# Four expert tiles at a time in L1_ffn, and another order of work in the attentions of a twelve-sublayer decoder

## The chip, the cores and the metric

The kernel runs on one core of one Trainium2 chip. TensorE (PE in the profile; PEld is its weight load) multiplies matrices, VectorE (DVE), ScalarE (ACT) and GpSimd (POOL) work on rows of 128 partitions, and SyncE (SP) issues most of the DMAs. The metric is the device time of one execution in microseconds; the kernel before takes 4104.81 us, the median of three runs (4103.65 to 4107.08).

## The reference

The input is 128 sequences of 64 tokens with 128 features, 8192 tokens. Twelve sublayers follow one another, each with the sum and a layer norm around it; everything is float32:

```
x = layernorm(x + sublayer(x))       # 12 times
```

They are, in order: a mixture of 8 experts (moe_first), a single-head cross attention, a feed-forward with ternary weights, the attention with rotary positions and a difference of two softmaxes (diff), a masked cross attention (causal), the mixture of 32 small experts (L1_ffn), the attention with distance biases (alibi), a cross attention with masked keys (keys), a convolution with experts, a gated scan, a cross attention with a full mask (full), and a mixture of 8 experts (moe_last). Five of them share one shape, 16 heads of 8 features over 64 tokens:

```
scores = einsum('bihd,bjhd->bhij', x @ Wq, ctx @ Wk) * scale     # masked or biased
probs  = softmax(scores, -1)
out    = einsum('bhij,bjhd->bihd', probs, ctx @ Wv).reshape(b, s, 128) @ Wo + bo
```

In diff queries and keys are first multiplied by rotary tables, values have 16 features for 8 pairs of heads, and what is normed by its root mean square and goes on is the first softmax's output less lambda times the second's. keys has no Wo. The mixture of small experts, with a hidden layer of 32:

```
e = argmax(x @ router_w.T + router_b)                  # one of 32 experts per token
y = relu(relu(x @ w1[e] + b1[e]) @ w2[e] + b2[e])
```

## The kernel before, in words

Nothing is scheduled by a program: each engine's instructions stand in the order in which the sublayer's function writes them (`body` in a block per engine), and semaphores alone tie the engines together. Sublayers don't overlap.

**Attention** (`attention`, L1047) goes through 16 chunks of 512 tokens, each of four tiles k = 0 to 3 of 128 tokens. Chunk c's tiles are computed while chunk c + 1 is projected, and the output of chunks c - 1 to c - 3 is finished. For tile t, TensorE's `body` (L1345) writes: `scores` of tile t + 1 (4 products on 64x64 quarters of the array, in four of the mask besides); `mix_values` of t - 1 (16 small products of probabilities with values); `turn(t, 0)` (four transposes of the probabilities into the bank pT); at some k a projection (`project` into the banks near and far), `turn_output` or `output`; `turn(t, 1)` into the same bank pT; at some k `project_values` (into near) and `turn_rows` (near). `turn(t, 1)` waits until ScalarE has copied what `turn(t, 0)` wrote. ScalarE's `body` (L1440) writes the copy of `turn(t, 0)`, the copy of `turn(t, 1)`, and both exponentials of tile t + 1 (`exponentials`, L1419). DVE's `body` (L1580) writes `shift_scores` of t + 1 (maximum and difference, twice), `heads_output` of t - 1, and at some k `rope_products` (only diff), `residual`, `moments` and `normalise`. POOL spreads keys over the blocks of heads (`spread_keys`, L1654) and does the small powers.

VP is the number of value projections per chunk: 1, and 2 in diff, where they stand behind tiles 1 and 2, and the rotary products behind tiles 0 and 1. In diff each chunk's output is also normed: ScalarE squares (`square_output`), DVE sums (`mean_squares`), POOL takes the power -1/2 (`rms`, L1677, L1691), and DVE multiplies (`rms_output`, L1556) at the start of the chunk after the next.

**L1_ffn** (`moe_small`, L2204) sorts the tokens by expert in two halves (parts). Each token gets a slot so that a tile of 128 slots has one expert; a half has 32 + 32 = 64 tiles. POOL scatters the rows to slots in DRAM (slot_x) and later gathers the results (slot_y). The loop in between takes a pair of tiles j, 64 pairs in all: SP and ScalarE each load one expert (161 columns: w1, its bias, and w2 with its bias as a 33rd row) into a ring of 8; SP loads the pair's rows three pairs ahead (`load_slots`) and stores the results (`store_slots`); TensorE writes `turn(j + 2)`, `hidden(j + 1)`, `output(j)`; ScalarE copies the transposes and does the first relu; DVE evicts. In L1_ffn the bank of the hidden layer is called rank_ps and that of the output count_ps. SP's part and TensorE's part of the loop:

```
for j in range(ALL):                                    # SP, L2402
    if j + 3 < ALL: load_expert(sp, 2 * (j + 3))
    if j + 3 < ALL: load_slots(j + 3)
    store_slots(j)                                      # waits for the eviction of j
for j in range(-2, ALL):                                # TensorE, L2473
    turn(j + 2); hidden(j + 1); output(j)
```

## Time and profile before

| | |
|---|---|
| median of 3 runs | 4104.81 us (4103.65 to 4107.08) |
| the profiled execution's own time | 4081.88 us |
| its span | 4080.1 us |
| busy in the span | PE 3018.0, PEld 2047.6, DVE 2256.7, ACT 1718.3, POOL 1789.2 us |
| mean granted clock of TensorE | 0.859 |

The profile shows one execution. Its own time lies 1.8 us over its span, and 23 us under the median of the other runs. Busy shares are means over twelve sublayers, so the views below are taken by stretch. A granted clock of 1.00 is 2.4 GHz and one of 0.50 is 1.2 GHz. In a row of the timeline an `x8` means that several like instructions in a row are told as one; a float32 product appears as two records. A name leaves its numbers out: L_ffn is L1_ffn in the stretch from 1753 to 2150 us. The stages that the change touches lie at 935 to 1405 us (diff), 1428 to 1738 (causal), 1753 to 2150 (L1_ffn), 2171 to 2481 (alibi), 2512 to 2824 (keys) and 3404 to 3714 (full).

### The profile page before, as it was taken

To read this page: it belongs to the slowest core of one execution; us is meant where nothing else is said; L and a number is where in the kernel's file an instruction comes from. 1 tells how busy PE (TensorE), PEld (TensorE's weight loads), DVE (VectorE), ACT (ScalarE), POOL (GpSimd) and SP (SyncE) were. 2 spreads that over 40 slices of the span, in tenths; PEclk is the share of its full clock that TensorE was granted. 3 is DMA by queue.
4 is the path that set the end of the run, shared out by engine and by line. 5 is a ranking of instruction groups with operands and counts; after the bars stand their busy time and mean duration, and the time that the engine had idled before them with its cause. 6 is when DMAs were issued, how large, how long until landed. Compare 5 with 4: busy or idle time off the path is not lost. (4 is left out here: it accounts for less than half of the span.)

```text
span 4080.1 us, 81328 instructions
## 1 busy us (share of the span) xinstructions
PE 3018.0 (74%) x27802; PEld 2047.6 (50%) x27802; DVE 2256.7 (55%) x6213; ACT 1718.3 (42%) x3334; POOL 1789.2 (44%) x1575
## 2 busy tenths in 40 slices
PE   3399907767777599946747996886899867997693
PEld 2387805554455356634524664554344434666572
DVE  2002336536777577751235775886777576775123
ACT  0144404334444366602214664664555554662341
POOL 2544272225565455523344554664022354552534
PEclk9999959888998799955558998998898788997896
DMA  6377611020010112114521112221000001221573
GB/s 215 115 227 218 191 41 45 6 7 24 32 41 31 53 55 73 55 41 122 136 76 41 55 53 67 76 86 59 1 1 1 1 3 47 77 67 56 160 224 106
DMA packets 305037, 304.44 MB, mean 75 GB/s; under 512 B 91108, under 2 KB 226821, under 8 KB 304648
## 3 DMA queue, kind: packets, MB, share of 16 engines
q1 hardware_dynamic: 269160, 252.01, 20.1%
q0 software_dynamic: 16384, 33.59, 2.8%
q10 hardware_dynamic: 19232, 15.50, 1.2%
q8 instruction: 147, 2.41, 0.2%
q14 instruction: 114, 0.93, 0.1%
HBM read 161.27 MB, written 55.84 MB: 53 GB/s over the span
## 5 line engine op out<-in xcount | busy, mean ns | idle before, releaser
L802 DVE TENSOR_TENSOR moe_first_tile_y<-moe_first_out_ps,moe_first_expert_w 128x256 f32<-128x256 f32 x78 | 33.1, 425 | 336.5 <-PE moe_first_out_ps L937 336.4
L998 POOL DMA_INDIRECT slot_x<-x_tok,moe_first_slots x128 | 123.7, 967 | 177.8 <-DVE moe_first_slots L775 75.1
L978 ACT ACTIVATE moe_first_hid<-moe_first_hid_ps,moe_first_expert_w 128x256 f32<-128x256 f32 x312 | 128.2, 471 | 155.6 <-PE moe_first_hid_ps L926 155.6
L1012 POOL DMA_INDIRECT moe_first_token_y<-slot_y,moe_first_slots x128 | 123.8, 967 | 100.4 <-issue 65.2
L1665 POOL TENSOR_TENSOR causal_k_blocks<-causal_k_T,headmask 128x1024 f32<-128x1024 f32 x64 | 121.2, 1896 | 105.9 <-PE causal_scores L1277 101.9
L2783 PE MATMUL L_ffn_experts<-L_ffn_expert_w,x_T 128*128 128x512 f32 x256 | 166.2, 735 | 1.8 <-ACT L_ffn_expert_out L2880 1.8
L1665 POOL TENSOR_TENSOR alibi_k_blocks<-alibi_k_T,headmask 128x1024 f32<-128x1024 f32 x64 | 121.2, 1896 | 105.2 <-PE alibi_scores L1277 101.2
L1665 POOL TENSOR_TENSOR full_k_blocks<-full_k_T,headmask 128x1024 f32<-128x1024 f32 x64 | 121.2, 1896 | 93.8 <-PE full_scores L1277 89.5
L937 PE MATMUL moe_first_out_ps<-moe_first_expert_w,moe_first_hid 128*128 128x128 f32 x1248 | 162.2, 281 | 0.0
L1416 ACT ACTIVATE diff_probs_T<-diff_pT 128x512 f32<-128x512 f32 x128 | 76.4, 597 | 183.0 <-PE diff_pT L1291 183.0
L1665 POOL TENSOR_TENSOR keys_k_blocks<-keys_k_T,headmask 128x1024 f32<-128x1024 f32 x64 | 120.7, 1896 | 74.7 <-PE keys_scores L1277 71.1
L937 PEld LDWEIGHTS moe_first_out_ps<-moe_first_expert_w,moe_first_hid 128*128 128x128 f32 x1248 | 150.8, 191 | 5.0 <-issue 0.2
L926 PE MATMUL moe_first_hid_ps<-moe_first_tile_xT,moe_first_expert_w 128*128 128x256 f32 x624 | 149.1, 382 | 0.6 <-ACT moe_first_tile_xT L969 0.6
L2338 DVE COPY L_ffn_tile_y<-L_ffn_count_ps 128x256 f32<-128x256 f32 x64 | 27.2, 425 | 195.8 <-PE L_ffn_count_ps L2466 195.8
L2946 POOL TENSOR_SCALAR L_ffn_ms_eps<-L_ffn_ms 128x4 f32<-128x4 f32 x16 | 3.7, 231 | 290.6 <-DVE L_ffn_ms L2713 290.6
L2705 DVE SCALAR_TENSOR_TENSOR L_ffn_combined<-L_ffn_expert_out,L_ffn_mix,L_ffn_combined 128x128 f32<-128x128 f32 x448 | 128.5, 349 | 4.0
L1665 POOL TENSOR_TENSOR diff_k_blocks<-diff_k_T,headmask 128x1024 f32<-128x1024 f32 x64 | 126.3, 1993 | 9.3 <-POOL diff_k_T L1652 5.6
L1416 ACT ACTIVATE keys_probs_T<-keys_pT 128x512 f32<-128x512 f32 x128 | 76.4, 597 | 114.7 <-PE keys_pT L1291 114.7
L2527 POOL DMA_INDIRECT slot_x<-x_tok,L_ffn_slots x64 | 66.8, 1044 | 131.2 <-DVE L_ffn_tile_y L2338 64.8
L1509 DVE TENSOR_REDUCE diff_maxima<-diff_scores 128x8 f32<-128x512 f32 x128 | 87.0, 680 | 65.0 <-PE diff_scores L1277 65.0
L1416 ACT ACTIVATE causal_probs_T<-causal_pT 128x512 f32<-128x512 f32 x128 | 76.4, 597 | 107.5 <-PE causal_pT L1291 107.5
L1416 ACT ACTIVATE alibi_probs_T<-alibi_pT 128x512 f32<-128x512 f32 x128 | 76.4, 597 | 107.2 <-PE alibi_pT L1291 107.2
(544 smaller groups left out, 9152.3 us busy)
## 6 DMA issues: line engine op xcount, KB each, us to landing
moe_first_expert_w<-in_L_attn_experts SPq DMA_DIRECT2D x78, 578.0 KB, 4.0
moe_last_expert_w<-in_L_ffn_experts SPq DMA_DIRECT2D x46, 578.0 KB, 4.1
slot_x<-blank ACTq DMA_DIRECT2D x2, 4992.0 KB, 44.2
moe_first_tile_x<-slot_x SPq DMA_DIRECT2D x78, 128.0 KB, 4.1
slot_y<-moe_first_tile_y SPq DMA_DIRECT2D x78, 128.0 KB, 1.9
L_ffn_tile_x<-slot_x SPq DMA_DIRECT2D x64, 128.0 KB, 2.3
slot_y<-L_ffn_tile_y SPq DMA_DIRECT2D x64, 128.0 KB, 1.8
moe_last_tile_x<-slot_x SPq DMA_DIRECT2D x46, 128.0 KB, 3.9
```

What stands on the lines that cost most here:

```text
L802: dve.tensor_tensor(y_out[:, q, :, :], out_bank[q][:, 0:SLOT_TILE].rearrange("p (s d) -> p s d", s=SPAN), over(wall[:, j % RING, 2 * FF + ...
L926: last = pe.matmul(hid_bank[h][:, SLOT_TILE * (b % 2):SLOT_TILE * (b % 2) + SLOT_TILE], wall[:, j % RING, 128 * b:128 * b + 128], xT[:, j ...
L937: last = pe.matmul(out_bank[j % 2][:, D * s:D * s + D], hid[:, j % 2, b, TILE * s:TILE * s + TILE], wall[:, j % RING, FF + D * b:FF + D * ...
L978: act.activation(hid[:, j % 2, b, :], hid_bank[b // 2][:, SLOT_TILE * (b % 2):SLOT_TILE * (b % 2) + SLOT_TILE], gelu, bias=wall[:, j % RIN ...
L998: pool.indirect_dma_start(slot_x[part][:, :], bass.IndirectOffsetOnAxis(slots[:, part, r, t:t + 1], 0), net.x_tok[:, part * K + t, :], Non ...
L1012: pool.indirect_dma_start(y_in[:, p, k, r, :], None, slot_y[part][0:NT * SLOT_TILE, :], bass.IndirectOffsetOnAxis(slots[:, part, r, t:t + ...
L1416: act.activation(probs_T[:, t.p, 4 * g:4 * g + 4, :].rearrange("p k t -> p (k t)"), pT_bank[:, :], ACT.Copy)\
L1509: dve.tensor_reduce(maxima[:, t.p, heads], src, AX_X, ALU.max).then_inc(max_done, 1)
L1665: pool.tensor_tensor(k_blocks[:, t.p, :, :], keys.to_broadcast([128, 8, TILE]), lanes.to_broadcast([128, 8, TILE]), ALU.mult).then_inc(spr ...
L2527: pool.indirect_dma_start(slot_x[part][:, :], bass.IndirectOffsetOnAxis(slots[:, part, t:t + 1], 0), net.x_tok[:, part * K + t, :], None). ...
L2705: last = dve.scalar_tensor_tensor(combined[:, p, k, :], expert_out[:, p, k, e, :], w, combined[:, p, k, :], ALU.mult, ALU.add)
L2783: pe.matmul(expert_bank[g][:, :], net.x_T[:, TILE * t:TILE * t + TILE], experts_s[:, 4 * g:4 * g + 4, :].rearrange("p e d -> p (e d)"), st ...
```

## The change

In all five attentions TensorE writes `turn(t, 0)` ahead of `mix_values(t - 1)`, and ScalarE writes the first exponentials of tile t + 1 right behind the copy of `turn(t, 0)`, the second ones behind the copy of `turn(t, 1)`. In diff the value projections stand behind tiles 2 and 3 instead of 1 and 2, and the product with the inverse root mean square is done by POOL right after its power, one chunk earlier than DVE did it.

In L1_ffn four tiles (a quad) are one step. Their four hidden layers are four products on the four column groups of the array (32 columns each) into one bank, their outputs four products on the four row groups (32 rows each) into four banks, with the second bias added by four more products of ones with a row group; one relu with 128 partitions and one eviction of 128x512 follow. An expert's weights come in two loads (w1: 128x32; w2 and biases: 32x257). Slot rows are loaded two quads ahead. The output's banks are no longer doubled: `output(j)` waits for the eviction of j - 1. Nothing else changes.

```diff
@@ attention @@
+    V_AT = PER - VP if lambdas is not None else PER - 1 - VP
@@ project_values, turn_output @@
-                    if wo is not None and c.shift(-2 - late).inside(CHUNKS) and n == VP - 1:
+                    if wo is not None and c.shift(-2 - late).inside(CHUNKS) and n == 0:
                         pe.wait_ge(oT_copied, done(c.shift(-2 - late)))
...
-                            pe.wait_ge(v_copied, nth(c.shift(2 + late), 2 * VP, 2))
@@ TensorE, body @@
                             scores(t.shift(1))
+                        turn(t, 0)
                         if t.shift(-1).inside():
                             mix_values(t.shift(-1))
-                        turn(t, 0)
...
-                        if PER - 1 - VP <= k < PER - 1 and c.shift(1).inside(CHUNKS):
-                            project_values(c.shift(1), k - (PER - 1 - VP))
+                        if 0 <= k - V_AT < VP and c.shift(1).inside(CHUNKS):
+                            project_values(c.shift(1), k - V_AT)
@@ ScalarE, body @@
                         copy_turned(t, 0)
+                        if t.shift(1).inside():
+                            exponentials(t.shift(1), 0)
...
                         copy_turned(t, 1)
                         if t.shift(1).inside():
-                            exponentials(t.shift(1))
+                            exponentials(t.shift(1), 1)
@@ DVE: rms_output and its calls are gone; POOL, rms @@
                     pool.tensor_tensor(rms_inv[:, :], ms_eps[:, :], minus_half[:, :], ALU.pow).then_inc(rms_done, 1)
+                    pool.wait_ge(rms_done, done(c))
...
+                    pool.tensor_tensor(o_heads[:, c.u % 2, :, :].rearrange("p t (k d) -> p (t k) d", k=8),
+                                       o_diff[:, c.u % 2, :, :].rearrange("p t (k d) -> p (t k) d", k=8),
+                                       spread_last(rms_inv[:, :], dv), ALU.mult).then_inc(o_normed, 1)
@@ moe_small @@
-    J = NT // 2
+    J = NT // 4
...
-    RING, XRING = 8, 4
+    RING, XRING = 4, 3
@@ DVE, evict @@
-                    dve.tensor_copy(y_out[:, q, :, :], out_bank[q][:, 0:PAIR].rearrange("p (s d) -> p s d", s=2))\
-                        .then_inc(out_done, 1)
+                    dve.tensor_copy(y_out[:, q, :, :], out_banks[:, :, 0:D]).then_inc(out_done, 1)
@@ load_expert @@
+                eng.dma_start(up[:, j % RING, g, :], w_up[bass.ds(e, 1), :, :].rearrange("o p h -> p (o h)"))\
+                    .then_inc(w_landed[j % RING], 16)
+                eng.dma_start(down[H * g:H * g + H, j % RING, :], w_down[bass.ds(e, 1), :, :].rearrange("o p w -> p (o w)"))\
+                    .then_inc(w_landed[j % RING], 16)
@@ SP @@
                 for j in range(ALL):
+                    if j + 2 < ALL:
+                        load_slots(j + 2)
                     if j + 3 < ALL:
-                        load_expert(sp, 2 * (j + 3))
+                        load_expert(sp, j + 3, 0)
+                    store_slots(j)
                     if j + 3 < ALL:
-                        load_slots(j + 3)
-                    store_slots(j)
...
+                        load_expert(sp, j + 3, 2)
@@ TensorE, hidden and output @@
+                    pe.wait_ge(w_landed[j % RING], 128 * (j // RING + 1))
+                    for g in range(4):
+                        last = pe.matmul(hid_bank[j % 2][H * g:H * g + H, 0:TILE], up[:, j % RING, g, :],
+                                         xT[:, j % 2, TILE * g:TILE * g + TILE], start=True, stop=True)
...
+                    if j >= 1:
+                        pe.wait_ge(out_done, j)
+                    for g in range(4):
+                        lane = slice(H * g, H * g + H)
+                        pe.matmul(out_banks[:, g, 0:D], net.ones[lane, :], down[lane, j % RING, D + 1:W], start=True, stop=False)
+                    pe.wait_ge(hid_done, j + 1)
+                    for g in range(4):
+                        lane = slice(H * g, H * g + H)
+                        last = pe.matmul(out_banks[:, g, 0:D], hid[lane, j % 2, :], down[lane, j % RING, 0:D],
+                                         start=False, stop=True)
@@ ScalarE, relu @@
+                    act.activation(hid[:, j % 2, :], hid_bank[j % 2][:, 0:TILE], ACT.Relu,
+                                   bias=down[:, j % RING, D:D + 1]).then_inc(hid_done, 1)
```

How the order moves, first on SP in the loop of L1_ffn. L_ffn_tile_x is a slot load, slot_y a store, L_ffn_expert_w (then _up and _down) an expert's weights; TENSOR_LOAD reads the expert's number. Before, one turn of the loop ends with the store and the next begins:

```order
L2376 DMA L_ffn_expert_w<-in_L_ffn_experts 128x161
L2389 DMA L_ffn_tile_x<-slot_x 128x2x128
L2395 DMA slot_y<-L_ffn_tile_y 128x2x128
L2375 TENSOR_LOAD L_ffn_expert_of
L2375 ISA x2
L2376 ISA
L2376 DMA L_ffn_expert_w<-in_L_ffn_experts 128x161
L2389 DMA L_ffn_tile_x<-slot_x 128x2x128
```

The same place after the change, a store of quad j and the slot load of quad j + 3 behind it:

```order
L2395 DMA slot_y<-L_ffn_tile_y 128x4x128
L2373 TENSOR_LOAD L_ffn_expert_of
L2373 ISA x2
L2374 ISA
L2374 DMA L_ffn_expert_up<-in_L_ffn_up 128x32
L2376 ISA
L2376 DMA L_ffn_expert_down<-in_L_ffn_down 32x257
L2389 DMA L_ffn_tile_x<-slot_x 128x4x128
```

The slot load stands behind a store in both; before it is that of pair j + 4 behind the store of j, now that of quad j + 3 behind the store of j, with two weight loads in between instead of one.

TensorE in that loop before, where L_ffn_turn_ps is `turn`, L_ffn_rank_ps `hidden` and L_ffn_count_ps `output`:

```order
L2442 MATMUL L_ffn_turn_ps<-ident,L_ffn_tile_x 128x128 x2
L2454 MATMUL L_ffn_rank_ps<-L_ffn_tile_xT,L_ffn_expert_w 32x128 x2
L2466 MATMUL L_ffn_count_ps<-L_ffn_expert_w,L_ffn_hid 128x128 x2
L2442 MATMUL L_ffn_turn_ps<-ident,L_ffn_tile_x 128x128 x2
L2454 MATMUL L_ffn_rank_ps<-L_ffn_tile_xT,L_ffn_expert_w 32x128 x2
```

And after:

```order
L2445 MATMUL L_ffn_turn_ps<-ident,L_ffn_tile_x 128x128 x4
L2456 MATMUL L_ffn_rank_ps<-L_ffn_tile_xT,L_ffn_expert_up 32x128 x4
L2465 MATMUL L_ffn_out_ps<-L_ffn_expert_down,ones 128x128 x4
L2469 MATMUL L_ffn_out_ps<-L_ffn_expert_down,L_ffn_hid 128x128 x4
L2445 MATMUL L_ffn_turn_ps<-ident,L_ffn_tile_x 128x128 x4
```

The order of the three steps is the same; the groups are four instead of two, and the bias group is new.

TensorE in causal, tile 2 of a chunk, before: causal_o_ps is the mixing, causal_pT the transposes of probabilities, causal_near_ps the transposes of the output and then the values' projection.

```order
L1277 MATMUL causal_scores<-causal_k_blocks,causal_q_T 64x512 x4
L1302 MATMUL causal_o_ps<-causal_v_blocks,causal_probs_T 64x18 x16
L1291 MATMUL causal_pT<-ident,causal_probs 128x128 x4
L1322 MATMUL causal_near_ps<-ident,causal_o_heads 128x128 x4
L1291 MATMUL causal_pT<-ident,causal_probs 128x128 x4
L1251 MATMUL causal_near_ps<-causal_wv,causal_cT_in 64x64 x16
```

And after:

```order
L1278 MATMUL causal_scores<-causal_k_blocks,causal_q_T 64x512 x4
L1292 MATMUL causal_pT<-ident,causal_probs 128x128 x4
L1303 MATMUL causal_o_ps<-causal_v_blocks,causal_probs_T 64x18 x16
L1322 MATMUL causal_near_ps<-ident,causal_o_heads 128x128 x4
L1292 MATMUL causal_pT<-ident,causal_probs 128x128 x4
L1252 MATMUL causal_near_ps<-causal_wv,causal_cT_in 64x64 x16
```

The mixing now stands between the two groups of transposes.

## Rows read from the trace of the kernel before

**Rows 1.** The page's first line.
```profile
span 4080.1 us, 81328 instructions
```

**Rows 2.** Busy time by stretch: us, PE, PEld, DVE, ACT, POOL, clock, DMA share, GB/s.
```profile
1428.00:1738.00 310.00, 286.36 (x4085) 192.55 (x4082) 239.16 (x564) 192.17 (x345) 158.06 (x108) 1.00 0.17 61
...
2512.00:2824.00 312.00, 268.61 (x3926) 172.97 (x3926) 248.13 (x564) 187.23 (x333) 187.32 (x123) 0.99 0.21 73
...
1853.00:2088.00 235.00, 187.23 (x672) 118.30 (x672) 50.94 (x168) 67.76 (x200) 70.33 (x78) 0.50 0.48 131
```

**Rows 3.** Waits, whole span: who waited for whom, us in total, times, longest.
```profile
PE keys_pT L1291 <- ACT keys_probs_T L1416: 39.9, 49, 0.9
...
PE causal_pT L1291 <- ACT causal_probs_T L1416: 20.8, 34, 0.8
PE alibi_pT L1291 <- ACT alibi_probs_T L1416: 20.8, 34, 0.8
PE full_pT L1291 <- ACT full_probs_T L1416: 20.8, 34, 0.8
```

**Rows 4.** Timeline, PE, one causal stretch: start us, us, instruction, [idle before].
```profile
1610.51 1.11 PE L1302 MATMUL causal_o_ps<-causal_v_blocks,causal_probs_T 128*64 128x18 f32 x32
1611.55 0.66 PE L1291 MATMUL causal_pT<-ident,causal_probs 128*128 128x128 f32 x4
1612.99 0.63 PE L1291 MATMUL causal_pT<-ident,causal_probs 128*128 128x128 f32 x4 [0.78 <-ACT causal_probs_T L1416]
1613.55 0.41 PE L1272 MATMUL causal_scores<-causal_mask_b,causal_ident_b 64*64 64x512 bf16 x4
1613.79 1.03 PE L1277 MATMUL causal_scores<-causal_k_blocks,causal_q_T 64*64 64x512 f32 x8
...
1622.73 0.63 PE L1291 MATMUL causal_pT<-ident,causal_probs 128*128 128x128 f32 x4
1623.20 0.60 PE L389 MATMUL causal_near_ps<-ident,causal_ln_out 128*128 128x128 f32 x4
```

**Rows 5.** Timelines of PE, DVE, POOL and ACT in one chunk of diff.
```profile
1230.58 1.97 PE L1251 MATMUL diff_near_ps<-diff_wv,diff_xT_in 128*64 128x128 f32 x16 [3.96 <-DVE diff_qk_parts L1500]
...
1216.13 2.17 DVE L1561 TENSOR_TENSOR diff_o_heads<-diff_o_diff,diff_rms_inv 128x512 f32<-128x512 f32 x1 [1.31 <-POOL diff_rms_inv L1691]
...
1233.72 3.75 POOL L1665 TENSOR_TENSOR diff_k_blocks<-diff_k_T,headmask 128x1024 f32<-128x1024 f32 x2 [0.38 <-POOL diff_k_T L1652]
...
1239.55 5.50 POOL L1691 TENSOR_TENSOR diff_rms_inv<-diff_ms_eps,diff_minus_half 128x32 f32<-128x32 f32 x1 [0.24 <-POOL diff_ms_eps L1684]
...
1238.93 1.24 ACT L1407 ACTIVATE diff_v_blocks<-diff_near_ps 64x512 f32<-64x512 f32 x2
```

**Rows 6.** Timeline, all engines, in the expert loop of L1_ffn.
```profile
1901.66 1.22 PE L2466 MATMUL L_ffn_count_ps<-L_ffn_expert_w,L_ffn_hid 33*128 33x128 f32 x4
...
1902.92 0.42 DVE L2338 COPY L_ffn_tile_y<-L_ffn_count_ps 128x256 f32<-128x256 f32 x1 [3.61 <-PE L_ffn_count_ps L2466]
...
1904.51 0.35 SPq L2376 DMA_DIRECT2D L_ffn_expert_w<-in_L_ffn_experts  x1
...
1904.90 0.43 SPq L2389 DMA_DIRECT2D L_ffn_tile_x<-slot_x  x1
...
1907.22 0.69 PE L2442 MATMUL L_ffn_turn_ps<-ident,L_ffn_tile_x 128*128 128x128 f32 x2 [1.26 <-DMA L_ffn_tile_x<-slot_x]
...
1907.84 1.06 PE L2454 MATMUL L_ffn_rank_ps<-L_ffn_tile_xT,L_ffn_expert_w 128*32 128x128 f32 x4
...
1908.83 0.58 PE L2466 MATMUL L_ffn_count_ps<-L_ffn_expert_w,L_ffn_hid 33*128 33x128 f32 x1
```

**Rows 7.** Tile L_ffn_count_ps: ns min/median/max, first and last start.
```profile
L2338 DVE COPY L_ffn_tile_y<-L_ffn_count_ps x64: 424/425/425, 1859.0 to 2087.6; 128x256 f32<-128x256 f32 x64
...
L2307 DVE COPY L_ffn_before_tile<-L_ffn_count_ps x4: 680/686/692, 1791.3 to 1822.6; 128x512 f32<-128x512 f32 x4
```

**Rows 8.** DMA issues: KB each, median us from issue to landing.
```profile
moe_first_tile_x<-slot_x SPq DMA_DIRECT2D x78, 128.0 KB, 4.1
```

More of the change, by code:

```diff
@@ L1461, in _ @@
                     copy_values(first.c, n)
[L1462 removed]
+                for g in range(2):
+                    exponentials(first, g)
                 chunk_turns(act, body)
```

158 lines of the change are left out of this document (66 added, 92 removed).

## The prediction

> **What bounds the kernel now.** I read the page first. Its busy shares are means over twelve sublayers that run one after the other on one core [rows 1], so they say little; the stretches of the five attentions and of the small-expert sublayer come next. In causal, a typical attention, TensorE is busy 286.4 of 310 us at a granted clock of 1.00, with DVE at 239.2: TensorE sets the pace. In keys it is 268.6 of 312 and DVE is nearer, 248.1. In the loop of L1_ffn the clock stands at 0.50 (1.2 GHz), the DMA engines are busy 0.48 of the time, and no engine is full [rows 2]. Then the waits. In causal, alibi, keys and full one wait of TensorE stands out: the second group of transposes waits for ScalarE's copy of the first (both go through one bank), 20.8 + 20.8 + 39.9 + 20.8 = 102.3 us in all [rows 3]. The timeline shows it: mixing starts at 1610.51, the first transposes at 1611.55, and the second ones only at 1612.99 after 0.78 us idle [rows 4]. In diff three things stop the chain: the projection of the next chunk's values waits 3.96 us for the rotary products on DVE, and everything behind it on TensorE waits too, scores included; DVE waits 1.31 us for POOL's power and then takes 2.17 us for the product with it [rows 5].
>
> In L1_ffn the timeline is to be read as a ring [rows 6]. Output of one pair starts at 1901.66. DVE evicts at 1902.92, SP stores, reads an expert's number, issues the expert's load at 1904.51 and the slot load at 1904.90; TensorE starts that load's transposes at 1907.22, having waited for it, the hidden layer at 1907.84 and the output at 1908.83. That is 7.17 us, and two pairs are done in it, since a slot load is issued three pairs ahead. 64 pairs [rows 7] took 235 us [rows 2].
>
> **Attention other than diff.** The mixing (1.04 us from start to start) moves in between the two transposes of a tile. A wait of 0.78 to 0.9 us is then covered whole, wherever it stood; the 102.3 us are the most that can go. What is late next: in causal, alibi and full DVE has 71 us of slack in 310 [rows 2], so I count all of 62.4. In keys DVE is busy 248.1 us, and with the gaps between its dependent instructions some 16.0 us of a chunk of 19; TensorE less its waits needs 16.6. I take 32 of the 39.9. The first transposes now follow the scores at once and so want their exponentials one mixing earlier. ScalarE gives them the first half right after its copy of the first transposes; the shifted scores of that half are ready two DVE instructions after the scores, some 1.4 us, while TensorE has 3.3 us or more of other work before it asks. I cost that at nothing; if DVE falls behind, it comes back tile by tile (rival 3).
> Against it stands one more change of the array's shape in each tile (scores, transposes, mixing, transposes, where it was scores, mixing, transposes). The row: four transposes followed by another full-size group take 0.47 us from start to start (1622.73 to 1623.20), followed by 64x64 ones 0.56 (1612.99 to 1613.55) [rows 4]. I take 0.07 of that difference of 0.09 for each of 5 x 64 tiles, 22 us; bounds 0 and 0.15 (48 us). The Trainium skill, TensorEngine Tiling (Array Packing), section Tiling Modes, says that a change of tiling mode drains TensorE; it gives no price, and these two rows agree in sign. Four sublayers: 62.4 + 32 - 4 x 4.5 = 76 us less; bounds 30 and 102.
>
> **diff.** Removed from DVE, per chunk: the product of 2.17 us and the wait of 1.31 us ahead of it [rows 5]; and, since the values are projected one tile later, TensorE no longer blocks the scores behind them, 3.96 us. Together 7.4 us. Given back, by following one chunk from the end R of its last rotary product: POOL adds the rotary parts and spreads keys (with R at 1230.5 its two spreadings run from 1233.72 to 1237.47; the first, needed for the next chunk's first scores, ends at about R + 5.2 [rows 5]), so these scores end at R + 6.2 while DVE is free at R + 5.4: 0.8 us. In tile 3 TensorE now projects the second half of the values and the transposes of the rows stand right behind it, in the same bank: they wait for ScalarE's copy of the transposes (0.6), an exponential (0.6) and the two copies of values (1.24) [rows 5], so that the following scores end at R + 13.3, where DVE was ready at R + 10.6: 2.7 us. POOL gets the product: a spreading of twice the size takes it 3.75 / 2 = 1.9 us [rows 5], so 0.9 to 1.9, and at most the 2.17 of DVE; I take 1.3. It stands behind the power of 5.50 us, and POOL's next keys come at about R + 16.5, just before TensorE asks at R + 17. Net 7.4 - 0.8 - 2.7 = 3.9 us in this chunk; as its waits are larger than the average (15 of 16 chunks wait), I take 2.8 x 15 = 42 us, less 4 for the change of shape: 38. Bounds: 0 (POOL or the new wait takes it all) and 4.5 x 15 = 68.
>
> **L1_ffn.** Work is halved in count: 32 quads for 64 pairs, one eviction, one slot load, one store, one relu each; two weight loads per tile instead of one. But the order of SP and TensorE closes the ring. SP issues the slot load of quad j + 2 after it has stored quad j - 1; TensorE transposes quad j + 2 directly after the output of quad j - 1. Nothing of TensorE's lies beside the way from output to output any more, and each turn of the ring does one quad. Its terms, at 1.2 GHz:
> - Eviction to slot load: 1904.90 - 1902.92 = 1.98, plus 0.27 for 128x512 instead of 128x256 (686 against 425 ns [rows 7]), plus 0.39 for the second weight issue (1904.90 - 1904.51) [rows 6]: 2.65.
> - Landing of the slot load: 2.32 for 128 KB (1904.90 to 1907.22) [rows 6]; 256 KB are bounded by that and by the 4.1 of the same size in the busier moe_first [rows 8]. I take 3.0.
> - Four transposes: 0.62 is two of them and 0.08 of hand-over [rows 6], so 1.16.
> - Hidden: 0.99 for 512 columns streamed now [rows 6]; 1024 columns, on four column groups. Unshared 2.0; shared in four 0.5. The scores, on four quarters of the array, stream 8 x 512 columns in 1.03 us at 2.4 GHz [rows 4], against 512 in 1.22 us at 1.2 GHz here: groups do run beside each other. I take 0.7.
> - Bias and output: 2048 columns on four row groups. Unshared 4.9 (four times 1.22), shared 1.2; I take 1.4.
> - Hand-overs 0.1.
> Sum 9.0 us a quad against 7.17 for the same four tiles. 29 quads wait in the ring (three loads are issued ahead), the first output and the last two quads add 14 us (three times three groups as above): 29 x 9.0 + 14 = 275 against 235, 40 us more. Bounds: with landing 2.32, hidden 0.5, output 1.2 the ring is 7.9, 243 us, 8 more; with 4.1, 2.0 and 4.9 it is 14.9, 446 us, 211 more. All else hides: ScalarE's four issues and two copies take some 4 us of each 9; POOL's scatter and gathers keep their pace.
> The Trainium skill speaks against this part too: TensorE: Matmul & The Clock Gate, section LDWEIGHTS, says that a weight load costs by its columns, not its rows, so a 32x128 load is as long as a 128x128 one. By its figure, the 16 loads of 128 columns take at least 16 x 107 ns = 1.7 us as an estimate, and the ring 9.3; my 1.4 would be 0.3 short, 9 us in all. No row here shows loads on four row groups.
>
> **Sum.** 4105 - 76 - 38 + 40 = 4031 us; against the profiled execution's own 4082 it would be 4008. That execution ran 23 us under the median of the three runs; I forecast against the median, as the changed kernel will be timed. I say **4030**.
>
> **Rivals.**
> 1. The ring is slower still, and the kernel with it. The groups of hidden and output don't run beside each other at these sizes, and the larger landing comes near 4. Place: the loop of L1_ffn. It decides from (235 + 114 - 14) / 29 = 11.6 us a quad, where the loop eats the 114 us of the attentions. At 14.9 the time is 4105 - 114 + 211 = 4202. For it: only 128 columns per instruction, all unshared bounds. Against: the scores' rows. Chance 0.11.
> 2. The ring isn't what binds: slot loads come in time as SP runs ahead. Then TensorE (3.3 us of groups) and ScalarE (some 4 us of copies and issues) set about 4.4 a quad, 32 x 4.4 + 6 = 147 us, 88 less: 4105 - 114 - 88 = 3903. Against: SP's store stands before the load and waits for the eviction. Chance 0.05.
> 3. The wait moves instead of going: the first transposes wait for exponentials, DVE is the bound, and the four attentions keep their 102 us. 4105 - 38 + 40 = 4107, less what little is saved: 4100. For: DVE at 0.8 of keys. Against: 71 us of slack in the other three. Chance 0.10.
> 4. diff gains nothing, POOL's 5.50 us and the product behind it being the new pace, or the new wait in tile 3 being longer: 4105 - 76 + 40 = 4069. Chance 0.14.
> The forecast itself 0.60, with a range of its own from 3985 to 4085.
>
> **From these to the numbers.** 0.2% is 8 us, about what a measurement can tell here from no change. Faster: 0.58 of the forecast, 0.05, 0.03 of rival 3, 0.13 of rival 4: 0.79. Same: 0.01 + 0.04 + 0.01 and 0.02 of rival 1: 0.08. Slower: the rest, 0.13. Range 3970 to 4110: it leaves out rival 2, most of rival 1 and the forecast's tails.
>
> **What would show it.** TensorE's wait in the second transposes (102.3 us) nearly gone, the four stretches some 15 to 30 us shorter each; no new wait of the first transposes for exponentials of more than a few us. In diff no 4 us wait at the projection of values, and a new one of 1 to 2 us at the transposes of the rows. In L1_ffn DMA waits ahead of every group of transposes, 5 us each, and quads 9 us apart. I am wrong if quads come faster than 7.2 us or slower than 11.6, or if a wait for exponentials fills the place of the old one.

## The result, and the profile after

The changed kernel takes **4087.6 us** (median of 5 runs, 4079.9 to 4091.0), the kernel before on the same chip 4107.0 (5 runs, 4103.7 to 4111.5): ratio 0.9949, interval 0.9935 to 0.9964, **19.4 us less** (15 to 27 by the interval). The forecast was 4030, some 75 us less. The sign was right and the time lies in the range, but three quarters of the gain are missing.

First the stretches, each from the start of an attention's first scores to that of its last. Columns: window, length, busy time (and instructions) of TensorE, its weight loads, DVE, ScalarE and POOL, TensorE's clock, DMA share, GB/s. Before, for causal, keys and diff:

```profile
1430.10:1729.80 299.70, 278.22 (x3976) 185.65 (x3972) 234.47 (x552) 186.44 (x336) 155.96 (x107) 1.00 0.18 62
2514.80:2815.20 300.40, 260.27 (x3808) 166.30 (x3804) 243.43 (x552) 181.17 (x323) 185.09 (x122) 1.00 0.22 74
938.60:1372.80 434.20, 342.64 (x3762) 216.57 (x3764) 336.14 (x688) 197.32 (x351) 258.40 (x147) 0.90 0.09 33
```

The same view after, with alibi, full and the loop of L1_ffn, which answers to the last of [rows 2]:

```profile
1416.70:1704.40 287.70, 281.03 (x3976) 185.66 (x3972) 232.50 (x549) 196.06 (x336) 154.72 (x107) 1.00 0.18 65
2524.00:2831.60 307.60, 274.90 (x3808) 169.51 (x3803) 281.92 (x548) 184.40 (x320) 182.92 (x121) 0.97 0.21 72
963.00:1363.50 400.50, 335.21 (x3766) 211.13 (x3764) 336.64 (x672) 201.20 (x351) 265.81 (x161) 0.94 0.10 35
2194.00:2481.20 287.20, 282.24 (x3972) 186.09 (x3972) 232.47 (x549) 194.54 (x335) 154.67 (x106) 0.99 0.14 51
3419.10:3707.70 288.60, 282.36 (x3972) 185.82 (x3971) 233.26 (x549) 198.94 (x336) 163.89 (x122) 0.99 0.22 67
1827.30:2111.00 283.70, 99.65 (x924) 64.59 (x924) 44.23 (x134) 35.03 (x71) 71.13 (x79) 0.50 0.36 92
```

Alibi and full took 299.3 and 299.9 before. By stretch the change is:

| stretch | before | after | difference | forecast |
|---|---|---|---|---|
| causal, alibi, full | 898.9 | 863.5 | -35.4 | -49 |
| keys | 300.4 | 307.6 | **+7.2** | -27.5 |
| diff | 434.2 | 400.5 | -33.7 | -38 |
| L1_ffn, first to last eviction | 228.6 | 275.1 | +46.5 | +40 |
| sum | | | -15.4 | -74.5 |

keys is the row that turned round: DVE's busy time there rose from 243.4 to 281.9 us with no instruction added. TensorE's rose too, from 260.3 to 274.9 us, at a granted clock of 0.97 for 1.00, so that its idle time fell (40.1 to 32.7 us) and the stretch still grew. The waits of keys after (who waited for whom: us, times, longest) show who is late now; TensorE's wait of 39.9 us for the copy of the transposes [rows 3] is down to 11.7, but ScalarE's exponentials wait for DVE:

```profile
ACT keys_probs L1422 <- DVE keys_probs L1515: 101.1, 97, 3.7
...
PEld keys_pT L1292 <- ACT keys_probs L1422: 36.6, 34, 1.6
...
DVE keys_maxima L1511 <- PE keys_scores L1278: 15.5, 8, 9.5
...
PE keys_pT L1292 <- ACT keys_probs_T L1416: 11.7, 19, 1.4
```

DVE's instructions in keys by line (busy us, mean ns of one, idle before) say which became longer. Before:

```profile
L377 DVE TENSOR_SCALAR keys_ln_out<-keys_resid_sum,keys_ln_moments,keys_ln_rstd 128x128 f32<-128x128 f32 x52 | 23.4, 509 | 0.0
...
L1578 DVE TENSOR_TENSOR keys_resid_sum<-keys_o_heads,keys_x_res 128x512 f32<-128x512 f32 x14 | 9.6, 687 | 2.0 <-DVE keys_o_heads L1545 2.0
```

After:

```profile
L1511 DVE TENSOR_REDUCE keys_maxima<-keys_scores 128x8 f32<-128x512 f32 x125 | 84.8, 678 | 15.9 <-PE keys_scores L1278 15.5
L377 DVE TENSOR_SCALAR keys_ln_out<-keys_resid_sum,keys_ln_moments,keys_ln_rstd 128x128 f32<-128x128 f32 x52 | 57.1, 1156 | 0.0
L1571 DVE TENSOR_TENSOR keys_resid_sum<-keys_o_heads,keys_x_res 128x512 f32<-128x512 f32 x14 | 21.1, 1504 | 2.1 <-DVE keys_o_heads L1547 2.1
```

Normalise grew by 33.7 us and the residual by 11.5, 45 together (DVE's busy time by 38.5, since its records overlap and the others got shorter). What reads scores from PSUM kept its time (691 and 678 ns, before 692 and 686). The timeline of one chunk (start, us, instruction) puts POOL's row of instructions beside it:

```profile
2692.34 3.75 POOL L1654 TENSOR_TENSOR keys_k_blocks<-keys_k_T,headmask 128x1024 f32<-128x1024 f32 x2
...
2695.15 4.36 DVE L377 TENSOR_SCALAR keys_ln_out<-keys_resid_sum,keys_ln_moments,keys_ln_rstd 128x128 f32<-128x128 f32 x4
...
2696.05 1.27 POOL L1664 TENSOR_TENSOR keys_x_res<-keys_x_in,keys_add_row 128x512 f32<-128x512 f32 x1
...
2697.27 1.90 POOL L1654 TENSOR_TENSOR keys_k_blocks<-keys_k_T,headmask 128x1024 f32<-128x1024 f32 x1
```

Four instructions that take 0.34 us each when free need 4.36 us, and end 0.34 us after POOL's run ends (2699.17). The Trainium skill has a rule for this: SBUF — State Buffer, section Who interferes with whom, says that DVE and GpSimd share one pair of SBUF ports as an exclusive lock, and that a VectorE tensor_scalar in a two-port mode, or an operation with two SBUF inputs beside a GpSimd instruction that reads SBUF, waits for the one that started first. These rows agree: 39 of the 52 normalise instructions overlap a spreading or the sum of the residual's input (keys_x_res) on POOL and take 0.61 to 1.93 us, the 13 that meet nothing take 333 to 335 ns.

The ring of L1_ffn after, from the output of one quad to that of the next (start, us, instruction); it answers to [rows 6]:

```profile
1965.15 0.65 PE L2469 MATMUL L_ffn_out_ps<-L_ffn_expert_down,L_ffn_hid 32*128 32x128 f32 x8
...
1965.87 0.69 DVE L2337 COPY L_ffn_tile_y<-L_ffn_out_ps 128x512 f32<-128x512 f32 x1 [8.05 <-PE L_ffn_out_ps L2469]
...
1968.62 0.60 SPq L2389 DMA_DIRECT2D L_ffn_tile_x<-slot_x  x1
...
1971.76 1.12 PE L2445 MATMUL L_ffn_turn_ps<-ident,L_ffn_tile_x 128*128 128x128 f32 x4 [5.96 <-DMA L_ffn_tile_x<-slot_x]
...
1972.81 0.66 PE L2456 MATMUL L_ffn_rank_ps<-L_ffn_tile_xT,L_ffn_expert_up 128*32 128x128 f32 x8
...
1973.39 0.81 PE L2465 MATMUL L_ffn_out_ps<-L_ffn_expert_down,ones 32*128 32x128 f32 x8
...
1973.98 0.65 PE L2469 MATMUL L_ffn_out_ps<-L_ffn_expert_down,L_ffn_hid 32*128 32x128 f32 x8
```

Output to output is 8.83 us, 9.0 was forecast. Only at the border of the two halves is it otherwise: the next eviction starts 15.2 us after this one, though its output is written 8.83 us after the last, and the profile names no instruction that it waits for.

```profile
1981.08 0.69 DVE L2337 COPY L_ffn_tile_y<-L_ffn_out_ps 128x512 f32<-128x512 f32 x1 [14.52 <-remote]
```

### The profile page after: what moved, and what is told of

Read it like the earlier page. It is cut to its first block and busy times, and to the rows that moved or that the text cites. A ratio compares the mean times of both kernels' runs of the same rounds, so it can differ in the third digit from the quotient of the medians.

```text
span 4086.8 us, 81776 instructions
## 1 busy us (share of the span) xinstructions
PE 2947.4 (72%) x28058; PEld 1992.9 (49%) x28058; DVE 2290.8 (56%) x6164; ACT 1721.7 (42%) x3206; POOL 1797.4 (44%) x1591
## 5 line engine op out<-in xcount | busy, mean ns | idle before, releaser
L937 PEld LDWEIGHTS moe_first_out_ps<-moe_first_expert_w,moe_first_hid 128*128 128x128 f32 x1248 | 154.0, 193 | 36.7 <-issue 16.3
L2445 PE MATMUL L_ffn_turn_ps<-ident,L_ffn_tile_x 128*128 128x128 f32 x128 | 35.6, 433 | 188.0 <-DMA L_ffn_tile_x<-slot_x 187.1
L2337 DVE COPY L_ffn_tile_y<-L_ffn_out_ps 128x512 f32<-128x512 f32 x32 | 22.1, 691 | 252.8 <-PE L_ffn_out_ps L2469 223.4
L2496 ACT ACTIVATE L_ffn_tile_xT<-L_ffn_turn_ps 128x512 f32<-128x512 f32 x32 | 19.1, 597 | 304.7 <-PE L_ffn_turn_ps L2445 288.0
L802 DVE TENSOR_TENSOR moe_last_tile_y<-moe_last_out_ps,moe_last_expert_w 128x256 f32<-128x256 f32 x46 | 19.5, 424 | 188.1 <-PE moe_last_out_ps L937 178.4
L1422 ACT ACTIVATE keys_probs<-keys_probs 128x512 f32<-128x512 f32 x128 | 80.7, 631 | 104.1 <-DVE keys_probs L1515 104.0
```

The source lines that it names most:

```text
L802: dve.tensor_tensor(y_out[:, q, :, :], out_bank[q][:, 0:SLOT_TILE].rearrange("p (s d) -> p s d", s=SPAN), over(wall[:, j % RING, 2 * FF + ...
L937: last = pe.matmul(out_bank[j % 2][:, D * s:D * s + D], hid[:, j % 2, b, TILE * s:TILE * s + TILE], wall[:, j % RING, FF + D * b:FF + D * ...
L1422: act.activation(e, e, ACT.Exp, scale=scale).then_inc(exped, 1)
```

## The experiments

Chips differ: the kernel before took 4105.4 us beside e1 to e4, 4070.2 beside e5 to e8, 4073.3 beside e9 to e12 and 4069.8 beside e13 and e14, so kernels of different groups are compared by their ratio to it (0.9949 for the change itself) and by their stretches. A ratio of 0.001 is 4.1 us. A good part of what differs lies in the unchanged moe_first, whose last transposes start at 529 to 534 us in e1 to e4 and at 497 to 507 us in e5 to e14.

**e1, the attentions alone** (the small-expert sublayer and its weights' layout as before).

> All the edits in the attentions, the small-expert sublayer as it was before (pairs of tiles). If the stretches of the two profiles add up as read, the ring of quads costs 47 us (loop 234 before, 282 after) and this kernel takes about 4087 - 47 = 4040 us, with the loop back at 234. Rival: the ring's cost is half returned elsewhere in the sublayer (its set-up, its tail), and this kernel takes 4060 or more. If it takes under 4030 the attentions brought what was forecast (-114) less only a little.

Measured: 4032.5 us, ratio 0.9822 (0.9798 to 0.9846), 73 us less than before. First to last eviction 229.2 us again. So the quads cost 0.0127 x 4105 = 52 us by the ratios (46 by the evictions), and the attentions brought 73, not 114. The expected 4040 holds within the interval (4022 to 4042).

**e2, keys in its old order.**

```diff
-                        turn(t, 0)
+                        if name not in ("keys",):
+                            turn(t, 0)
                         if t.shift(-1).inside():
                             mix_values(t.shift(-1))
+                        if name in ("keys",):
+                            turn(t, 0)
```

Both exponentials of keys stand after the second copy again.

> The changed kernel, but with keys in its old order (mixing ahead of both groups of transposes, both exponentials after the second copy). Theory: in keys the new order moves DVE's normalise and residual (SBUF to SBUF) beside POOL's spreading, where they take 1156 and 1504 ns on average in place of 509 and 687, 45 us of DVE time in all. So here keys takes 300 us again instead of 308, normalise 0.51 us, and the kernel 4080 us (7 less than the changed kernel). Rival: keys is slower for another reason that the neighbours bring with them (layout in memory, clock): then 308 us stay and the time is 4087.

Measured: ratio 0.9935 (0.9914 to 0.9957), 4082.0 us; keys 300.2 us, normalise 517 ns, the residual 686. Stretch and durations are as before; the loss comes from the order in keys. The whole kernel's difference to the changed one lies inside the intervals, so this rests on the stretch: keys takes 302.3 to 308.3 us in the seven runs that have its new order and the mask in its old place.

**e3, the mask of keys made earlier.**

```diff
                         if k == 2 and c.shift(1).inside(CHUNKS):
-                            if moving_mask:
+                            if moving_mask and name not in ("keys",):
                                 make_mask(c.shift(1))
...
                             spread_keys(t.shift(2))
+                        if k == 0 and moving_mask and name in ("keys",) and c.shift(1).inside(CHUNKS):
+                            make_mask(c.shift(1))
```

> The changed kernel, but in keys POOL makes the next chunk's mask (1.94 us) in tile 0 after its spreading, not in tile 2 ahead of it. Theory: it is this 1.94 us, stacked with two spreadings and the bias row, that lies beside DVE's normalise in tile 2 and holds it for up to 4.36 us; moved away, normalise falls to 0.35 to 0.5 us (from 1.16), keys to 285 to 290 us like causal, alibi and full, and the kernel to 4065 to 4070 us. Rival: DVE in keys is held by the exponentials or its own sum of work (rival 3 of the prediction); then normalise may become short but keys stays above 300 us and the time at 4085 to 4090.

Measured: 4043.3 us, ratio **0.9836** (0.9812 to 0.9860). DVE's lines in keys now, and the stretch:

```profile
L377 DVE TENSOR_SCALAR keys_ln_out<-keys_resid_sum,keys_ln_moments,keys_ln_rstd 128x128 f32<-128x128 f32 x52 | 14.4, 340 | 0.0
...
L1571 DVE TENSOR_TENSOR keys_resid_sum<-keys_o_heads,keys_x_res 128x512 f32<-128x512 f32 x14 | 9.6, 686 | 2.1 <-DVE keys_o_heads L1547 2.1
```
```profile
2525.10:2787.50 262.40, 260.93 (x3804) 166.38 (x3804) 230.64 (x549) 190.96 (x320) 184.34 (x121) 1.00 0.25 84
```

keys fell by 45.2 us, the kernel by 44, twice what I expected. Of the 45.2, 31.2 are TensorE's idle time (32.7 to 1.5) and 14.0 its busy time, which is 260.9 us again at a clock of 1.00. The floor was misjudged: I took causal's 288 as the floor, but keys has no output projection, and TensorE's own 260.9 us are its floor. Against before the new order now saves 38.0 us in keys, nearly the whole wait of 39.9. The same work at another place of POOL's row is worth 45 us. POOL's mask delays its spreadings too, but TensorE waited only 2.1 us for them in keys after the change, and 2.3 here; it is DVE's time that went. full has such a mask in the same place, but one that takes POOL 0.62 us and not 1.94, and its normalise took 354 ns after the change, 341 before.

**e4, the ring opened.**

```diff
-    RING, XRING = 4, 3
+    RING, XRING = 4, 4
-                    if j + 2 < ALL:
-                        load_slots(j + 2)
+                    if j + 3 < ALL:
+                        load_slots(j + 3)
```

> The changed kernel with four buffers for slot rows in place of three, and the slot load issued three quads ahead in place of two. Theory: the 9.0 us from output to output then cover two quads, so that a quad takes 4.5 us or what SP's and ScalarE's issues allow, some 5; the loop falls from 282 to 160 to 190 us and the kernel to 3965 to 3995 us. Rival: the weight loads or the DMA queues bind next at 7 us or more a quad: the loop 225 us or more, the kernel 4030 or more.

Measured: 3965.7 us, ratio **0.9649** (0.9625 to 0.9673). The 32 evictions lie between 1831.1 and 1992.5 us: 161.4 in place of 275.1.

```profile
L2337 DVE COPY L_ffn_tile_y<-L_ffn_out_ps x32: 660/692/693, 1831.1 to 1992.5; 128x512 f32<-128x512 f32 x32
```

One more load ahead lets two quads share the way round. The ring was the bound. At 5.2 us a quad TensorE still waits 42.3 us for slot rows (21 times).

**e5 and e14, both mended** (e3's and e4's edits; the same kernel twice).

> The changed kernel with both earlier edits: the mask of keys made in tile 0 after the spreading, and slot rows loaded three quads ahead into four buffers. The two places lie in different sublayers, so the two gains should add: 4087.6 - 44 - 122 = 3921 us. Rival: one of them holds only because the clock or the DMA queues were in another state; then the sum falls short by 20 us or more (3941 or above).

> The kernel with both places mended, once more, as the measure for the run above: 0.954 of the kernel before, causal 287.7 us, diff 397.

Measured: 3883.0 us, ratio **0.9539** (0.9521 to 0.9557), and 3869.0, ratio 0.9505 (0.9492 to 0.9518). From e3 and e4 one expects 0.9836 x 0.9649 / 0.9949 = 0.9539. The gains add, and this kernel beats both. That one kernel comes to 0.9539 on one chip and 0.9505 on another, 14 us apart with intervals that don't meet, also says how far ratios of different chips can be trusted.

**e6, the kernel before with the mask made earlier.**

> The kernel before, with the one edit that in keys the mask is made in tile 0 after the spreading. Theory: before the change DVE's normalise in keys was held a little (509 ns against 341 in causal, some 9 us in all) and TensorE's wait for the copy of the transposes (39.9 us) set the pace, so moving the mask alone brings 0 to 9 us: keys 291 to 300, the kernel 4096 to 4105. Rival: the place of the mask is worth its 40 us with any order of TensorE: then keys is at 262 and the kernel at 4065.

Measured: ratio 0.9995 (0.9982 to 1.0008). Normalise falls to 342 ns, keys stays at 300.1 us, TensorE's wait for the copy at 38.2. The mask's place costs nothing while another wait sets the pace; only the new order makes it the bound.

**e7, normalise ahead of the shift in causal.**

```diff
+                        if name == "causal" and k == 2 and c.shift(-2 - late).inside(CHUNKS):
+                            tail.normalise(dve, c.shift(-2 - late))
                         if t.shift(1).inside():
                             shift_scores(t.shift(1))
```

> The changed kernel, but in causal DVE normalises in tile 2 ahead of the shift of that tile's scores, not after the output of the heads. No mask is made there by POOL; the place is chosen so that normalise starts when the scores end, as POOL's spreading (1.90 us) does. Theory: normalise (SBUF to SBUF) waits for POOL's spreading wherever the two meet: it rises from 341 ns to 600 to 900 on average (one of four stretched by up to 1.9 us, 14 chunks, some 15 to 27 us of DVE time). DVE has 44 us of waits for scores in causal, so the stretch grows by less, 0 to 15 us. Rival: what stretched it in keys was the mask alone (int32 to bf16): then 341 ns stay.

Measured: ratio 1.0075 (1.0060 to 1.0091); causal 354.3 us, 66.6 more, far from my 0 to 15. Normalise rose to 975 ns, in a sublayer whose mask is never made on POOL, so the lock is between normalise and the float operations of POOL. One chunk:

```profile
1576.55 3.66 DVE L377 TENSOR_SCALAR causal_ln_out<-causal_resid_sum,causal_ln_moments,causal_ln_rstd 128x128 f32<-128x128 f32 x4
...
1576.74 1.91 POOL L1656 TENSOR_TENSOR causal_k_blocks<-causal_k_T,headmask 128x1024 f32<-128x1024 f32 x1 [0.42 <-PE causal_scores L1278]
1578.61 1.26 POOL L1666 TENSOR_TENSOR causal_x_res<-causal_x_in,causal_add_row 128x512 f32<-128x512 f32 x1
```

The price was missed because I set the 33 us of DVE against its slack. This normalise stands between scores and their shift, so its 3.66 us (of which some 1.1 would be its own, unheld) go into the exponentials, and from there into ScalarE's copy of the outputs, for which the projection of values waits (5.6 us in the changed kernel). The wait adds 41.8 us; the other 24.8 are TensorE's busy time, 305.9 us for 281.0, at a granted clock of 0.89 for 1.00:

```profile
PE causal_near_ps L1252 <- ACT causal_o_T L1435: 47.4, 14, 3.7
```
```profile
1386.80:1741.10 354.30, 305.86 (x3976) 197.50 (x3971) 264.98 (x549) 194.05 (x336) 155.52 (x107) 0.89 0.15 53
```

**e8 to e11, diff and the order taken apart.** e8 puts the product with the power back on DVE. e9 projects diff's values one tile earlier, as before. e10 and e11 move one of TensorE's mixing and ScalarE's first exponential alone, in all five attentions, with e3's mask.

> The changed kernel, but in diff the product with the power is on DVE again, as before; the later values and all else stay. Theory: in the changed kernel POOL's product slows DVE's combination of heads (743 ns against 409, 60 times, 20 us), which gives back most of what DVE got rid of (31 us and its wait of 21), so undoing it costs little: diff 405 to 415 us against 400, the kernel 4090 to 4100. Rival: the product on POOL is what the gain of diff (34 us) comes from: 425 us or more, the kernel 4112.

> The changed kernel, but in diff the values are projected one tile earlier again, as before, with the waits that belong to it; the product stays on POOL. The prediction put 3.96 us a chunk on the wait of the projection for the rotary products, less what comes back: 0.8 and 2.7. Theory: moving the values brings most of what the product's move (some 12 to 16 us of the stretch by the run with the product back on DVE) doesn't: diff 34 us in all, so here about 415 to 420 us against 400. Rival: the two parts overlap (either alone gives nearly all): 400 to 405.

> The changed kernel with the mask of keys made early (TensorE's bound in keys visible), and ScalarE's exponentials together after the second copy, as before; TensorE's order is the new one. Theory: the wait for the copy is gone, but the first transposes follow the scores at once and their exponential stands behind the second copy, so a wait of 0.3 to 1 us a tile comes in its place: causal 295 to 325 us, keys 270 to 300, in place of 288 and 262. Rival: ScalarE has time enough and the spreading of exponentials does nothing: 288 and 262 stay.

> The changed kernel with the mask of keys made early, ScalarE's exponentials spread as in the changed kernel, but TensorE's mixing ahead of both groups of transposes, as before. Theory: TensorE meets the copy of the first transposes right behind them, and that copy is now followed by an exponential, not by the second copy's work; the wait of 20.8 us (39.9 in keys) stays or grows: causal 299 to 303, keys 298 to 302. Rival: the exponentials' place is what helps: under 292 in causal.

Measured, in us of the stretch (an empty cell is as in the changed kernel, within 2.2 us):

| kernel | diff | causal | alibi | keys | full | ratio (interval) |
|---|---|---|---|---|---|---|
| before | 434.2 | 299.7 | 299.3 | 300.4 | 299.9 | 1 |
| changed, e3 in keys | 396.7 | 287.7 | 286.4 | 262.4 | 288.7 | 0.9836 (0.9812 to 0.9860) |
| e8, product on DVE | 413.0 | | | | | 0.9961 (0.9947 to 0.9976) |
| e9, values as before | 403.5 | | | | | 0.9912 (0.9896 to 0.9929) |
| e10, mixing alone | 414.0 | 290.7 | 289.4 | 267.5 | 292.1 | 0.9868 (0.9848 to 0.9889) |
| e11, exponentials alone | 401.0 | 306.6 | 305.2 | 300.5 | 307.3 | 1.0048 (1.0029 to 1.0066) |

Nine runs whose diff is the changed one give 395.3 to 401.1 us there, median 396.8. Undoing one part costs 16 us (product), 17 (exponentials), 7 (values, 2.4 above the slowest of the nine) and 4 (mixing, inside their spread, so not told from nothing). The parts overlap, as they sum to 44 and the whole gain is 37. In e9 TensorE's wait of 4 us for the rotary products is back in full (49.5 us, 15 times), and still only 7 us come back: the rival held, not my 415 to 420.

In e10 causal and keys came out 3 and 5.5 us above the rival's figures and below the theory's; in e11 keys is as told and causal 4 us above. In the four other attentions moving the mixing brings 8 to 10 us of 11 to 13 (33 of 38 in keys), and the exponentials the rest; alone they cost 0 to 7 us. In e11 TensorE still waits 20.4 us for the copy in causal, and 6.1 more for ScalarE's copy of the outputs (before: none).

The theory I gave for e8 was wrong in its reason: DVE's combination of heads takes 702 ns with the product on DVE too (743 after, 409 before), so it is not the product on POOL that slows it. The trace has what does: this combination reads SBUF twice, and it is held where it meets POOL's spreading, as normalise is in keys. Before, 4 of 61 were held (1.18 to 1.26 us), after, 18 of 60 (0.55 to 1.92); all others take 0.35. The longest of them:

```profile
1012.72 1.92 DVE L1534 SCALAR_TENSOR_TENSOR diff_o_diff<-diff_o_pairs,diff_neg_lam 128x128 f32<-128x128 f32 x1
```
```profile
1012.60 3.80 POOL L1654 TENSOR_TENSOR diff_k_blocks<-diff_k_T,headmask 128x1024 f32<-128x1024 f32 x2
```

Normalise rose in diff too, from 340 to 590 ns (340 in e9, so it comes with the later values). Together that is 32 us, as much as the product took (31.3), and DVE's busy time in diff stayed at 336 us. Each of e8 to e11 has the combination above 700 ns, so undoing one part alone doesn't take it back.

The 16 us of the stretch are not all to be seen in e8's ratio, 0.0012 above that of the change, with intervals of 0.0015 on either side, and e9's ratio is 0.0037 below the change's with a diff 7 us longer. So kernels taken on different chips are not told apart to better than some 15 us; the stretches are.

**e12, pairs with a load four ahead** (the small-expert sublayer of before, XRING 5 for 4, the slot load issued four pairs ahead; the attentions as changed).

> The attentions as changed, the small-expert sublayer in pairs of tiles as before, but with five buffers for slot rows in place of four, and the slot load four pairs ahead in place of three. Theory: the ring of before let two pairs through in 7.17 us; with one more ahead it is three, 2.4 to 3 us a pair, if SP's issues (four per pair) allow: the loop falls from 235 to 155 to 195 us, the kernel from 4032.5 (the attentions alone) to 3955 to 3995, and quads bring nothing that the loads further ahead don't. Rival: another thing binds the pairs (ScalarE's issues, the eviction, weights that land late), and the loop stays above 215; then the quads are needed for the 162 us.

Measured: ratio 0.9695 (0.9677 to 0.9712), against 0.9822 for e1; the 64 evictions take 180.7 us (1808.0 to 1988.7) in place of 229.2. The theory holds within its window. The quads keep 19 us over such pairs (161.4), a sixth of the 114 that one more load brings them.

**e13, the copy of the outputs ahead of the exponential** (on both mended).

```diff
                         copy_turned(t, 0)
+                        if k == 2 and wo is not None and c.shift(-1 - late).inside(CHUNKS):
+                            copy_output(c.shift(-1 - late))
                         if t.shift(1).inside():
                             exponentials(t.shift(1), 0)
...
-                        if k == 2 and wo is not None and c.shift(-1 - late).inside(CHUNKS):
-                            copy_output(c.shift(-1 - late))
```

> The kernel with both places mended, and in tile 2 ScalarE copies the transposed outputs ahead of the first exponential in place of behind it. Theory: TensorE's wait for this copy at the projection of values (5.6 us in causal, alibi and full each, 16.5 in diff) goes, and nothing takes its place: causal 282 to 284 in place of 287.7, diff 381 to 390 in place of 397, the kernel 15 to 30 us under the one without the edit. Rival: the copy itself waits for TensorE's transposes of the outputs, which stand behind the mixing; the exponential then comes a mixing later, the first transposes of the next tile wait for it, and nothing is gained or some us are lost.

Measured: ratio 0.9583 (0.9570 to 0.9596), against 0.9505 for e14 on the same chip: slower. Causal is 287.7 us as in e14, its wait unmoved:

```profile
PE causal_near_ps L1252 <- ACT causal_o_T L1435: 5.6, 14, 0.4
```

The wait is 0.4 us a chunk at either place, and 5.6 us in e10 too, with no exponential ahead of the copy. Between the transposes of the outputs and the values TensorE now has only the second transposes (0.66 us), and the copy takes 0.69. Before, it also waited for the other copy ahead of the second transposes, and had no wait for this one; that the one hid the other is my reading. In diff the wait falls from 15.8 to 4.9, but the one for POOL's spread keys rises from 30.1 to 40.0, and diff takes 409.7 us for e14's 400.3. The rival's outcome came, nothing gained. The profiled executions are 11.8 us apart (3890.1 and 3878.3), and diff is 9.4 of that; the medians are 29 apart, and where the rest of that comes from no profile shows.

## Why the prediction was right or wrong

**The wait of TensorE in the four attentions: right in mechanism.** It vanished in causal, alibi and full, and in keys as soon as nothing else was late (38.0 us saved in e3).

**"I count all of 62.4": over-counted.** TensorE's idle time in causal fell from 299.7 - 278.2 = 21.5 us to 287.7 - 281.0 = 6.7, by 14.8, not 20.8. The rest is the wait of 5.6 us for the copy of the outputs, which was not there before; e10 and e13 show that it isn't the exponential's place that causes it. The change of the array's shape can have cost no more than the 2.8 us by which TensorE's busy time rose (4.5 taken; 0.7 in keys in e3). So 12.0 for 16.3, three times.

**"In keys ... I take 32 of the 39.9 ... I cost that at nothing; if DVE falls behind, it comes back tile by tile": the step that failed.** I looked at DVE's 248 us of 312 as a fixed sum and asked only if its order left room. The sum itself grew by 38.5 us with the same instructions, since the new order shifts DVE against POOL, and TensorE's busy time by 14.6 at a clock of 0.97 for 1.00. This is rival 3's mechanism in one sublayer of four, with a cause it didn't name. [Rows 2] had the hint: POOL was busy 187 us in keys and 158 in causal. The row of normalise, 509 ns in keys against 341 in causal, would have told it, and I hadn't read it. e2, e3 and e6 show the place, e7 the hold with no mask. Worth 35 us of the 59 between the two sums; the three other attentions are 14, the ring 6.5, diff 4.

**diff, -38: right in sum by luck, wrong in parts.** The stretch fell by 33.7 here and by 37.4 in the median of nine. But I booked it on the values' wait (3.96 a chunk) and the product (3.48), with a loss of 4 for the order. The runs give some 7 us to the values, 16 to the product and 17 to the spread exponentials, which I had not credited in diff at all; the mixing's 4 lie within the spread. The product's 2.17 us, which I took for DVE's own work, were themselves mostly a hold: all 14 started while POOL was spreading keys and ended 0.55 us after that instruction, and POOL does the same product in 1.06 us. What DVE was freed of, its held combination and normalise took back (32 us), the same fault as in keys. The wait at the transposes of the rows came as told (17.6 us, 12 times), one for the copy of the outputs came that I had not (16.2), and TensorE's wait for POOL's spread keys came to 28.4 us, where I had 0.8 a chunk.

**L1_ffn, +40: right in mechanism, 6.5 short.** The terms, in us, forecast and measured: eviction to slot load 2.65 and 2.75, landing 3.0 and 3.14, transposes 1.16 and 1.05, hidden 0.7 and 0.58, bias and output to the eviction 1.4 and 1.31. Groups on rows and columns of the array do run beside each other: the hidden layers' 1024 columns took 0.58 us, where 512 took 0.99 before. The 4.1 that I set as the upper end of the landing was for 128 KB, so it bounds nothing for 256. The stretch rose by 46.5 (52 by e1's ratio); the turn across the two halves took 15.2 us, 6.4 more than the 8.8 of those ahead of it, and the sum had no term for it. The estimate from the Trainium skill, TensorE: Matmul & The Clock Gate, section LDWEIGHTS, 1.7 us for 16 loads in a row, is not borne out: bias and output with all their loads took 1.31 at 1.2 GHz.

**The sum.** -35.4 + 7.2 - 33.7 + 46.5 = -15.4, measured -19.4, which the interval allows. The profiled executions compare otherwise (span 4080.1 before, 4086.8 after), because in the unchanged moe_first the same loop took 27 us longer in the one after. The runs above show that loop at either length with the changed attentions, so it is not the change's doing. That is why the sum goes by stretches.

## What to carry to other kernels

Before counting a removed wait as gain, look for short instructions of DVE with a mean above their minimum (here normalise in keys, 509 ns for 332, and the combination in diff, 409 for 350). Here each long one stood beside a POOL instruction, and the new order made the means 2.3 and 1.8 times as long. Read a ring of loads by what stands between two turns of it; a buffer more can be worth more than half the instructions (114 us here against 19). And take a total apart even when it comes out right, since in diff the parts were wrong.

## What the runs showed of the hardware

POOL's making of the mask (one int32 input, bf16 output) did not hold DVE's residual, which has two SBUF inputs. In e3, 13 of the 14 residuals start while a mask is being made, 1.1 to 1.7 us into it, and all 14 take 680 to 692 ns:

```profile
2644.82 0.68 DVE L1571 TENSOR_TENSOR keys_resid_sum<-keys_o_heads,keys_x_res 128x512 f32<-128x512 f32 x1
```
```profile
2643.75 1.94 POOL L1627 TENSOR_SCALAR keys_mask_b<-keys_mask_in 128x512 bf16<-128x512 int32 x1
```

Beside POOL's spreading (two float inputs) the same residual takes 2.31 us in the changed kernel:

```profile
2681.52 2.31 DVE L1571 TENSOR_TENSOR keys_resid_sum<-keys_o_heads,keys_x_res 128x512 f32<-128x512 f32 x1 [0.48 <-DVE keys_o_heads L1547]
```
```profile
2681.39 1.90 POOL L1654 TENSOR_TENSOR keys_k_blocks<-keys_k_T,headmask 128x1024 f32<-128x1024 f32 x1 [3.92 <-PE keys_scores L1278]
```

So in keys the mask did its harm by where it put the spreadings, not by itself: no normalise overlaps it there in the changed kernel. POOL's power in diff holds nothing either, with two float inputs and 5.4 us: the 14 combinations that fall into it after the change take 350 to 353 ns, as here:

```profile
1055.42 0.35 DVE L1534 SCALAR_TENSOR_TENSOR diff_o_diff<-diff_o_pairs,diff_neg_lam 128x128 f32<-128x128 f32 x1
```
```profile
1051.68 5.45 POOL L1680 TENSOR_TENSOR diff_rms_inv<-diff_ms_eps,diff_minus_half 128x32 f32<-128x32 f32 x1 [0.24 <-POOL diff_ms_eps L1673]
```

The Trainium skill, SBUF — State Buffer, section Who interferes with whom, says that a DVE instruction with two SBUF inputs contends with a GpSimd instruction that reads SBUF; for the mask and the power the traces show none of it. What sets these two apart, no run here tells. Open too is which part of the new order moves diff's combination beside the spreading.
